# First layer's reciprocal as a ScalarE seed with two Newton steps, the key cap read from PSUM, and a scan and a transpose placed later

## What is computed

```
xn = layernorm(x)
xm = xn * time_mix + shift(xn) * (1 - time_mix)
k, v, r = xm @ Wk, xm @ Wv, xm @ Wr
k  = exp(min(k, 60));  kv = k * v
wkv = causal_conv(kv, w);  wk = causal_conv(k, w) + 1e-9     # w decays by exp(-exp(decay)) per step
s = (sigmoid(r) * (wkv / wk)) @ Wo
h = s0 * ([xn, -xn] @ sign(k0));  h = 2 * relu(h)
h = 2 * relu(s1 * (h @ sign(k1)));  g = silu(s2 * (h @ sign(k2)))
x = x + s * g
```

## Time and profile before

| what | value |
|---|---|
| median of 3 runs | 672.55 us (672.5 to 673.92) |
| the profiled execution | 672.1 us |
| its span, first to last instruction | 670.3 us |
| granted PE clock, mean | 0.997 |
| busy share PE / DVE / ACT / POOL | 94% / 90% / 76% / 42% |
| start of `xm` in the bodies 0, 1, 2, 3, 15 | 10.5, 24.6, 44.0, 59.1, 245.4 us |

### The profile page before, as it was taken

How to read it: one execution, slowest core, us unless ns; L and a number is a source line. 1 busy time by engine, 2 the same in 40 slices (tenths; PEclk the granted TensorE clock), 3 DMA queues, 4 the chain that set the end, 5 groups by cost and what they waited for, 6 DMA issues and landing times. The chain is left out here.

```text
span 670.3 us, 9285 instructions
## 1 busy us (share of the span) xinstructions
PE 629.5 (94%) x2714; PEld 304.2 (45%) x2714; DVE 601.0 (90%) x1406; ACT 511.4 (76%) x794; POOL 280.1 (42%) x275
## 2 busy tenths in 40 slices
PE   4779999999999998799999999999999999999986
PEld 2334444444444443344545444454444544444442
DVE  4999999999999999988988988898898899889856
ACT  2846666666666665889988898898888889899886
POOL 6556777777777765222123032122313303221220
PEclk9999999999999999999999999999999999999999
DMA  7331000000000000000000000000000000000000
GB/s 178 109 94 31 1 0 1 1 0 1 0 2 1 0 1 1 1 0 1 16 1 17 17 4 14 16 17 0 17 17 1 17 17 17 0 18 17 0 17 32
DMA packets 10770, 11.65 MB, mean 17 GB/s; under 512 B 4800, under 2 KB 6288, under 8 KB 10720
## 3 DMA queue, kind: packets, MB, share of 16 engines
q1 hardware_dynamic: 9744, 10.73, 5.3%
q0 software_dynamic: 112, 0.33, 0.1%
q10 hardware_dynamic: 864, 0.00, 0.1%
HBM read 6.87 MB, written 4.19 MB: 16 GB/s over the span
## 5 line engine op out<-in xcount | busy, mean ns | idle before, releaser
L1150 PE MATMUL bank<-arena,w 128*128 128x512 f16 x640 | 148.6, 379 | 4.1 <-DVE arena L774 4.1
L1150 PE MATMUL bank<-arena,dnT 128*128 128x512 f32 x288 | 138.6, 592 | 0.0
L435 POOL TENSOR_TENSOR arena<-arena 128x512 f32<-128x512 f32 x48 | 59.7, 1271 | 137.6 <-ACT arena L590 137.6
L650 ACT ACTIVATE arena<-bank,xinv 128x512 f32<-128x512 f32 x144 | 94.4, 693 | 24.9 <-PE bank L1150 24.6
L1150 PEld LDWEIGHTS bank<-arena,w 128*128 128x128 f16 x640 | 62.5, 98 | 78.3 <-issue 10.1
L482 ACT ACTIVATE arena<-bank 128x512 f16<-128x512 f32 x96 | 53.8, 606 | 35.8 <-PE bank L1150 35.8
L425 POOL TENSOR_TENSOR arena<-arena 128x512 f32<-128x512 f32 x16 | 16.8, 1050 | 140.6 <-DVE arena L1011 140.6
L1150 PEld LDWEIGHTS bank<-arena,dnT 128*128 128x128 f32 x288 | 53.7, 191 | 35.9 <-issue 24.4
L1150 PE MATMUL bank<-arena,wsqT 128*128 128x512 f32 x128 | 64.6, 609 | 5.3 <-DVE arena L783 5.3
L1020 DVE SCALAR_TENSOR_TENSOR arena<-bank,cws,arena 128x506 f32<-128x506 f32 (+1 forms) x96 | 67.1, 740 | 1.1
L774 DVE SCALAR_TENSOR_TENSOR arena<-bank,arena 128x512 f16<-128x512 f32 x96 | 60.3, 671 | 2.4 <-ACT arena L482 1.2
(11 more groups left out here) (221 smaller groups left out, 1492.6 us busy)
## 6 DMA issues: line engine op xcount, KB each, us to landing
x_all<-in_L_attn_x SPq DMA_DIRECT2D x16, 256.0 KB, 2.6
out<-x_all SPq DMA_DIRECT2D x16, 256.0 KB, 2.0
up_n<-in_L_ffn_routed_up SPq DMA_DIRECT2D x1, 512.0 KB, 3.7
dn_n<-in_L_ffn_routed_down SPq DMA_DIRECT2D x1, 512.0 KB, 5.3
wx<-in_L_attn_W_x SPq DMA_DIRECT2D x1, 288.0 KB, 2.9
k_u<-in_L_ffn_k POOLq DMA_DIRECT2D x1, 256.0 KB, 5.8
w_in<-in_L_attn_W_in SPq DMA_DIRECT2D x1, 256.0 KB, 2.7
k_u<-in_L_ffn_k SPq DMA_DIRECT2D x1, 128.0 KB, 6.1
```

Of the source, the lines that this page charges most:

```text
L435: g.tensor_tensor(prod[:, c, :], act[:, c + 1, :], gate[:, :], ALU.mult).then_inc(sem["b_actp"], 1)
L650: a.activation(act[:, c, :], up_bank(f, c)[:, :], ACT.Gelu, scale=xinv[:, I_UP:I_UP + 1]).then_inc(sem["b_act"], 1)
L1150: return nc.tensor.matmul(ps, lhsT, rhs, start=start, stop=stop)
```

## The change

The two DVE reciprocals per body go. ACT makes a seed of 1/wk from the bits of `wk` read as an integer, `rec = exp(bits * SEED_SCALE + SEED_BIAS)`, and copies `wk` into bank b_F. DVE then makes `t1 = rec * wk` into bank b_S, `rec = (t1 - 2.00045) * rec`, `t2 = rec * wk` into b_S, and `ya = (t2 + 2) * ysr`; POOL makes `ysr = ysr * rec` between. The sign that two such steps leave is taken up by `c3[:, 3]` in `sg`. `ek` stays in b_K, and `ekm` is read from there. The `Pv` scans go behind `gp`, and on PE the turning back of `sg` goes behind `hidden1` block 1. POOL no longer makes `ya`; its product, and with it the normalisation behind it, waits for the first Newton step instead of for the whole reciprocal. The same is done in `last_hidden`.

```diff
+LOG2 = math.log(2.0)
+SEED_SCALE = -LOG2 / 2 ** 23
+SEED_BIAS = LOG2 * (127 - 0.043)
+NEWTON = 2.00045
...
@@ -175,7 +180,6 @@
 
 
         xm = tile(0, [P, N])
-        ek = tile(0, [P, N])
         ekm = tile(0, [P, N])
...
@@ -398,13 +403,14 @@
                     for j in range(POOLED):
                         pool.wait_ge(sem["a_hi1"], FC * m + j + 1)
                         g.tensor_tensor(hl[:, 1, j, :], relu[:, j, :], hh[:, 1, j, :], ALU.subtract).then_inc(sem["a_low"], 1)
-                    pool.wait_ge(sem["a_rec"], m + 1)
+                if has(m):
+                    pool.wait_ge(sem["a_r1"], m + 1)
                     pool.wait_ge(sem["a_ysr"], m + 1)
-                    after(pool, sem["a_s"], m)
-                    g.tensor_tensor(ya[:, :], ysr[:, :], rec[:, :], ALU.mult).then_inc(sem["a_y"], 1)
+                    g.tensor_tensor(ysr[:, :], ysr[:, :], rec[:, :], ALU.mult).then_inc(sem["a_q"], 1)
                 if has(f) and has(f + 1):
                     normalise(f + 1, "a_")
                 if has(f):
+                    after(pool, sem["a_y"], f)
                     pool.wait_ge(sem["a_wkc"], f + 1)
                     pool.wait_ge(sem["a_scanK"], f + 1)
                     g.tensor_tensor(seqs(wk[:, :]), seqs(wkc[:, :]), Pk[:, :, 0:T], ALU.add).then_inc(sem["a_wk"], 1)
@@ -503,12 +509,19 @@
                     if f == 0:
                         channel_factors()
                 if has(m):
+                    actv.wait_ge(sem["a_wk"], m + 1)
+                    after(actv, sem["a_q"], m)
+                    a.activation(rec[:, :], wk[:, :].bitcast(mybir.dt.int32), ACT.Exp, scale=SEED_SCALE,
+                                 bias=seedb[:, :]).then_inc(sem["a_rec"], 1)
+                    after(actv, sem["a_gp"], m)
+                    a.activation(b_F[:, :], wk[:, :], ACT.Copy).then_inc(sem["a_wkp"], 1)
+                if has(m):
                     high(1, m, 0)
                     high(1, m, 1)
                 if has(f):
                     actv.wait_ge(sem["a_k"], f + 1)
                     after(actv, sem["a_ekm"], f)
-                    a.activation(ek[:, :], b_K[:, :], ACT.Exp).then_inc(sem["a_ek"], 1)
+                    a.activation(b_K[:, :], b_K[:, :], ACT.Exp).then_inc(sem["a_ek"], 1)
                 if f == 1:
                     bounds()
                 if has(m):
@@ -561,6 +574,13 @@
 
             def last_hidden():
 
+                m = G - 1
+                actv.wait_ge(sem["a_wk"], m + 1)
+                actv.wait_ge(sem["a_q"], m)
+                a.activation(rec[:, :], wk[:, :].bitcast(mybir.dt.int32), ACT.Exp, scale=SEED_SCALE,
+                             bias=seedb[:, :]).then_inc(sem["a_rec"], 1)
+                actv.wait_ge(sem["a_gp"], m)
+                a.activation(b_F[:, :], wk[:, :], ACT.Copy).then_inc(sem["a_wkp"], 1)
                 high(1, G - 1, 0)
                 high(1, G - 1, 1)
                 up_high(0)
@@ -765,8 +785,33 @@
                 dve.wait_ge(sem["chan_ready"], 3)
                 dve.wait_ge(sem["const_done"], 1)
                 v.tensor_scalar(c3[:, 2:3], c3[:, 1:2], 0.5, None, ALU.mult)
+                v.tensor_scalar(c3[:, 3:4], c3[:, 1:2], -0.5, None, ALU.mult)
                 v.tensor_scalar(dec[:, 0:P], ones[:, :], tch[:, 1:2], None, ALU.mult)
                 v.tensor_scalar(dec[:, P:T], ones[:, 0:T - P], tch[:, 1:2], None, ALU.mult).then_inc(sem["const_done"], 1)
+
+            def first_product(n):
+
+                dve.wait_ge(sem["a_rec"], n + 1)
+                dve.wait_ge(sem["a_wkp"], n + 1)
+                after(dve, sem["a_sg"], n)
+                v.tensor_tensor(b_S[:, :], rec[:, :], b_F[:, :], ALU.mult).then_inc(sem["a_t1"], 1)
+
+            def first_step(n):
+
+                dve.wait_ge(sem["a_t1"], n + 1)
+                v.scalar_tensor_tensor(rec[:, :], b_S[:, :], NEWTON, rec[:, :], ALU.subtract, ALU.mult).then_inc(sem["a_r1"], 1)
+
+            def second_product(n):
+
+                dve.wait_ge(sem["a_r1"], n + 1)
+                v.tensor_tensor(b_S[:, :], rec[:, :], b_F[:, :], ALU.mult).then_inc(sem["a_t2"], 1)
+
+            def second_step(n):
+
+                dve.wait_ge(sem["a_t2"], n + 1)
+                dve.wait_ge(sem["a_q"], n + 1)
+                after(dve, sem["a_s"], n)
+                v.scalar_tensor_tensor(ya[:, :], b_S[:, :], 2.0, ysr[:, :], ALU.add, ALU.mult).then_inc(sem["a_y"], 1)
 
             def low(layer, n, j):
 
@@ -798,27 +843,28 @@
                     if ahead:
                         row_moments(sem["a_stat"])
                 if has(m):
-                    dve.wait_ge(sem["a_wk"], m + 1)
-                    after(dve, sem["a_y"], m)
-                    v.reciprocal(rec[:, 0:N // 2], wk[:, 0:N // 2])
+                    first_product(m)
+                    first_step(m)
+                    second_product(m)
                 if has(t):
                     dve.wait_ge(sem["a_sgT"], t + 1)
                     v.tensor_tensor(xs_of(t), xs_of(t), b_RX[:, :], ALU.add).then_inc(sem["a_x1"], 1)
                 if has(f):
                     dve.wait_ge(sem["a_ek"], f + 1)
                     after(dve, sem["a_wkc"], f)
-                    v.tensor_scalar(ekm[:, :], ek[:, :], math.exp(K_CAP), None, ALU.min).then_inc(sem["a_ekm"], 1)
+                    v.tensor_scalar(ekm[:, :], b_K[:, :], math.exp(K_CAP), None, ALU.min).then_inc(sem["a_ekm"], 1)
                     dve.wait_ge(sem["a_ekm"], f + 1)
                     dve.wait_ge(sem["a_v"], f + 1)
                     after(dve, sem["a_kvc"], f)
                     v.tensor_tensor(kv[:, :], ekm[:, :], b_V[:, :], ALU.mult).then_inc(sem["a_kv"], 1)
+                if has(m):
+                    second_step(m)
                 if f == 0:
                     for j in range(FC):
                         low(0, 0, j)
                     decays()
                     dve.wait_ge(sem["const_done"], 2)
                 if has(m):
-                    v.reciprocal(rec[:, N // 2:], wk[:, N // 2:]).then_inc(sem["a_rec"], 1)
                     low(1, m, 2)
                     low(1, m, 3)
                 if has(f):
@@ -829,6 +875,15 @@
                     last.then_inc(sem["a_scanK"], 1)
                 if f == 1:
                     largest()
+                if has(f) and f != 0:
+                    low(0, f, 0)
+                    low(0, f, 1)
+                    low(0, f, 2)
+                    low(0, f, 3)
+                if has(m):
+                    dve.wait_ge(sem["a_thf"], m + 1)
+                    after(dve, sem["a_sg"], m)
+                    v.scalar_tensor_tensor(gp[:, :], thf[:, :], 1.0, b_F[:, :], ALU.add, ALU.mult).then_inc(sem["a_gp"], 1)
                 if has(f):
                     dve.wait_ge(sem["a_kv"], f + 1)
                     after(dve, sem["a_wkv"], f)
@@ -836,19 +891,11 @@
                         last = v.tensor_tensor_scan(Pv[:, s, 1:], dec[:, :], kv[:, s * T:(s + 1) * T], 0.0,
                                                     ALU.mult, ALU.add)
                     last.then_inc(sem["a_scanV"], 1)
-                if has(f) and f != 0:
-                    low(0, f, 0)
-                    low(0, f, 1)
-                    low(0, f, 2)
-                    low(0, f, 3)
-                if has(m):
-                    dve.wait_ge(sem["a_thf"], m + 1)
-                    after(dve, sem["a_sg"], m)
-                    v.scalar_tensor_tensor(gp[:, :], thf[:, :], 1.0, b_F[:, :], ALU.add, ALU.mult).then_inc(sem["a_gp"], 1)
+                if has(m):
                     dve.wait_ge(sem["a_gp"], m + 1)
                     dve.wait_ge(sem["a_s"], m + 1)
                     after(dve, sem["a_sgT"], m)
-                    v.scalar_tensor_tensor(sg[:, :], b_S[:, :], c3[:, 2:3], gp[:, :], ALU.mult, ALU.mult).then_inc(sem["a_sg"], 1)
+                    v.scalar_tensor_tensor(sg[:, :], b_S[:, :], c3[:, 3:4], gp[:, :], ALU.mult, ALU.mult).then_inc(sem["a_sg"], 1)
 
             def magnitudes():
 
@@ -956,15 +1003,15 @@
                 dve.wait_ge(sem["bn_done"], G + 1)
                 row_moments(sem["b_stat"])
                 halves(w_inH[:, :], w_inL[:, :], w_in[:, :], col(wsc, I_IN)).then_inc(sem["prep_in"], 1)
-                dve.wait_ge(sem["a_wk"], m + 1)
-                dve.wait_ge(sem["a_y"], m)
-                v.reciprocal(rec[:, 0:N // 2], wk[:, 0:N // 2])
+                first_product(m)
+                first_step(m)
                 normalised(0, "b_")
+                second_product(m)
                 dve.wait_ge(sem["a_sgT"], m)
                 v.tensor_tensor(xs_of(m - 1), xs_of(m - 1), b_RX[:, :], ALU.add).then_inc(sem["a_x1"], 1)
-                v.reciprocal(rec[:, N // 2:], wk[:, N // 2:]).then_inc(sem["a_rec"], 1)
                 low(1, m, 2)
                 turned_low(0)
+                second_step(m)
                 low(1, m, 3)
                 up_low(0)
                 up_low(1)
...
@@ -1190,6 +1237,7 @@
```

(29 more changed lines are left out.)

## The result

The changed kernel takes 669.31 us (median of 14 runs, 668.48 to 671.48), the kernel before in the same series 673.62 (14 runs): a ratio of 0.9949, with a 95% interval of 0.9936 to 0.9963. It is faster, by 3.4 us by this ratio (4.3 by the medians) and not by the 9.5 forecast, and its time lies outside the forecast range, which ended at 668.0. The profiled execution has a span of 667.1 us after 670.3.

A forecast was written before the change was run, and what follows sets the result against it. PE was taken as the bound once the ring through POOL opens: 7.3 us from bodies 3 to 14, plus 0.2, 0.3, 1.3 and 0.4, make 9.5; 672.55 - 9.5 is 663.0 us, range 660.5 to 668.0.

The forecast's parts named there:

- PE's floor of 14.75 to 14.91: Steady body: 14.91 us if PE never stands, 14.75 if its matmuls also overlap more tightly; the change leaves PE's work alone.
- the sum of 7.3 us for bodies 3 to 14: Steady bodies: twelve go from 15.52 to 14.91 us each, saving 7.3 us.
- The ring from the reciprocal to `xn`: Steady body: POOL waits for the second reciprocal, PE for `xn`; opening it removes PE's 0.61 us wait per body.
- 14.54: Steady body: DVE's forecast work in us after the change, 0.37 below PE's floor.
- the first rival: Steady body: DVE stays the bound, POOL's earlier normalisation holding a `Pk` scan by 0.94 us; 669.9 us, chance 0.13.
- half a hold: Steady body: the first rival's `Pk` scan held by half of 0.94 us, giving bodies of 15.0 and 664.2 us.
- PE is the bound: Steady body: the main forecast, PE setting 14.8 to 15.1 us a body, chance 0.77.
- The products, the cap, ACT's work: Steady body: four DVE products take 2.64 us, the cap 0.72; ACT's added 1.2 is covered by its wait for PE.
- The moves: Steady body: turning back moves past one 1.72 us PE block, as `sg` comes 1.17 later; the delay costs nothing.
- The rest: Outside the steady bodies: savings of 0.2 us in body 2, 0.3 in body 1, 1.3 in body 15, 0.4 in the weave.
- 0.4 of 0.7: Weave into the second layer: reciprocals of 3.33 us become 2.64, some spent waiting for the last hidden block; 0.4 saved.
- Body 15: Last body: 16.16 goes to 14.9 us, saving 1.3, as its idle 1.1 goes and scans follow POOL's addition.

The follow-up runs named there:

- scan first: Changed kernel, with POOL's last normalisation step (`xn`) waiting for the `Pk` scans: 668.36 us, ratio 0.9916 to the kernel before.
- the first experiment: Changed kernel, with POOL's second addition of body 1 waiting until DVE has finished the chain of scales: 664.33 us, ratio 0.9884 to the kernel before.

## Why the prediction was wrong, point by point

**PE's floor of 14.75 to 14.91 and the sum of 7.3 us for bodies 3 to 14**: right in size, 7.6. The mechanism was half right. The ring from the reciprocal to `xn` did open: PE no longer waits for `xn`. But the `Pk` pair was held by 0.66 in each body, and a new ring through it and POOL set 14.88. DVE's list without that hold was 14.2 and not 14.54 (14.88 - 0.66): the first two low parts, `gp` and `sg` step at 1.19, 0.60 and 0.64 in their new places, and at 1.33, 0.72 and 0.74 before. With 14.54 the same hold would have made 15.2. The hold was the first rival's timing ("its last part ends about 193.1, while the `Pk` scans start near 192.0"), priced at half a hold with 15.0, and it ran beside the forecast, not against it. That the forecast's "PE is the bound" gave the right length is luck: the ring of 14.88 happens to be as long as the floor it named, and PE's own floor is 14.70.

**The products, the cap, ACT's work**: 2.65 for 2.64, 0.72 for 0.72, and the exponential no later. Right.

**The moves**: in the steady body they cost nothing, as said; the old places cost 0.8 (turning back) and 1.6 (scans) a body. Outside it the moved scans are the loss of body 1, whose chain takes 5.08 with the moves alone and 5.07 in the changed kernel, and part of the weave's. The prediction weighed the moves for the steady body only.

**The rest**: this step failed. It took bodies 1 and 2 and the weave as DVE's own work with a saving subtracted, "0.2", "0.3" and "0.4 of 0.7"; the changed kernel's trace has +1.7 for body 1, +1.5 for body 2 and +3.1 for the weave. It asked which POOL instruction now lies beside which DVE instruction only for the steady body and for body 15. With the `Pv` scans moved, POOL's additions, product and low parts come in an unbroken row over the chain of scales (before, it waited 1.25 and 1.04 ahead of its two low parts there), and with the shorter division POOL's product follows its low parts at once over the normalisation of the weave. The trace of before had the price at hand: one instruction of 128x1 elements in that chain took 1.05 us there already. And it left out the consequence for PE, whose clock was low behind its longer idle times: 1.5 to 2 us more in body 2, 1.6 in the weave. Without these falls the held instructions alone cost 1.7 in body 1 and about 1.5 in the weave. Why the clock falls in one execution and not in another after the same idle time is open, and with it how much of the loss each execution pays.

**Body 15**: near in size, 1.7 for 1.3, by another way than told. Its idle time didn't go: the 0.94 ahead of the cap did, but DVE then waits 0.38 for POOL's product and 0.69 for low part 3. What was won is the hold of the `Pv` pair (2.19 to 1.27), the division and the cap.

## What to carry to other kernels

When an instruction is moved or an engine relieved of a wait, list what the instructions behind it on other engines will now run beside, also in the first and last passes, which the sum over the steady loop doesn't see: here they took back more than half of a gain that was forecast to 0.3 us. Where two engines hold each other's instructions, a wait added on the one with slack (at three places here) can be worth more than work removed from the full one. And an idle time of PE costs twice if its clock falls behind it; look at the granted clock by stretch, not at its mean, and before a stretch of one trace is compared with another's, see that both have the same clock.

## What the runs showed of the hardware

- A `tensor_scalar` of 128x7 elements on DVE takes 0.16 us with POOL idle and 0.93 to 1.00 beside POOL's 128x512 instructions, and a `tensor_tensor` of 128x1 takes 0.16 or 1.22; the four 128x128 normalising instructions take 1.11 or 3.43. A held instruction ends as POOL's does: 42.78 beside 42.77 in the chain. The Trainium skill (SBUF — State Buffer, "Who interferes with whom") says the same of two-port modes and of two SBUF inputs, and the rows agree for both: `tensor_scalar` on SBUF, and the scans. Not every small instruction is held: two `tensor_scalar` of 128x1 in the chain (42.90 and 43.94) took 0.15 while POOL was busy.
- After 4.24, 4.08 and 3.92 us of idle time (changed kernel, moves only, scan first) PE's clock was at its lower level in body 2, after 0.80 and 1.13 it wasn't. In between it went both ways: after 2.99 the weave's eight matmuls took 3.47 in the changed kernel, after 2.98 they took 1.89 in the first experiment; after 2.25 and 2.24 ahead of body 1 four f32 matmuls took 1.98 and 2.90. The length of the idle time alone doesn't decide it.
- DVE's products that write a bank step at 0.61, and at 0.72 where the next one needs them, as those that write SBUF do.
